# Attention's first unit: a fourth pair of score banks, and the third half of scores ahead of the feed-forward's last transposes

## The reference

```python
x = x + 0.5 * ffn(layernorm(x))
x = x + attention(layernorm(x))
x = x + 0.5 * ffn(layernorm(x))

# ffn: 8 experts, the best 2 of each token by sigmoid score plus bias, and a shared expert
h      = square(relu(score * (xf @ w_up.T)))     # hidden width 176 for each expert
hs     = square(relu(xf @ shared_w_up.T))
out    = sum of the two experts' h @ w_down.T + hs @ shared_w_down.T

# attention: one head, 4096 fixed keys and values
q      = hidden @ Wq.T + bq
scores = q @ memory_keys.T / sqrt(128)
probs  = softmax(scores)
out    = (probs @ memory_values) @ Wo.T + bo
```

## Time and profile before

| | us |
|---|---|
| median of 3 runs | 653.56 |
| the three runs | 653.99, 653.56, 652.54 |
| the profiled execution, its own time | 654.36 |
| its span, first to last instruction | 652.6 |

### The profile page before, as it was taken

One profiled execution on the slowest core, in us unless ns is written; L12 is line 12 of the kernel. 1 busy time (PEld: TensorE's weight loads), 2 busy tenths in 40 slices (PEclk: granted clock), 3 DMA queues, 4 the chain that ended last, 5 costly groups with the idle time before them and its releaser, 6 DMA issues.

```text
span 652.6 us, 9400 instructions
## 1 busy us (share of the span) xinstructions
PE 612.6 (94%) x2868; PEld 432.5 (66%) x2884; DVE 531.6 (81%) x944; ACT 455.9 (70%) x765; POOL 398.3 (61%) x443
## 2 busy tenths in 40 slices
PE   7799998798989999999999999999999988999997
PEld 4455544576767777777777777777777766645543
DVE  5889886886967978988887897897898858699885
ACT  3577787474757777777777776777776765567886
POOL 4987670462565966867677587596677787524100
PEclk9899999899989999999999999999999999999999
DMA  8021210425264373653735727447355360000000
GB/s 308 6 64 34 65 33 1 113 58 137 59 153 102 92 162 86 141 118 81 174 82 129 158 61 170 95 99 171 81 138 109 87 130 1 1 17 17 33 32 33
DMA packets 35857, 59.19 MB, mean 91 GB/s; under 512 B 9056, under 2 KB 9696, under 8 KB 35680
## 3 DMA queue, kind: packets, MB, share of 16 engines
q1 hardware_dynamic: 31936, 53.34, 34.2%
q10 hardware_dynamic: 3360, 4.21, 2.5%
q0 software_dynamic: 512, 1.05, 0.6%
HBM read 8.23 MB, written 2.10 MB: 16 GB/s over the span
## 4 chain that ended last, share of the span: by engine, by line
PE 64%; DVE 19%; issue 5%; ACT 4%; SPq 3%; POOL 2%; DMA 1%; ACTq 1%; DVEq 0%; POOLq 0%
PE banks L1400 7%; PE banks L1402 7%; PE banks L1401 7%; PE banks L1441 6%; PE banks L1443 6%; PE banks L1442 6%; PE banks L1261 4%; DVE bank_max L1123 4%; PE banks L1420 4%; PE banks L1252 4%; DVE probsT L1019 4%; DVE E L1118 3%; SPq L351 3%; PE banks L1451 2%; PE banks L1271 2%
## 5 line engine op out<-in xcount | busy, mean ns | idle before, releaser
L551 POOL TENSOR_TENSOR p_lo<-probsT,p_hi 128x768 fp32r<-128x768 f32 (+1 forms) x128 | 226.9, 1776 | 129.1 <-ACT p_hi L759 128.7
L1123 DVE TENSOR_REDUCE bank_max<-banks 128x1 f32<-128x1024 f32 x128 | 156.0, 1219 | 33.4 <-PE banks L1402 32.4
L1400 PE MATMUL banks<-kv_lo,q_parts 128*128 128x512 f32 x256 | 112.4, 439 | 10.2 <-ACT E L781 5.1
L759 ACT ACTIVATE p_hi<-probsT 128x768 fp32r<-128x768 f32 (+1 forms) x128 | 104.3, 816 | 24.0 <-PE banks L1443 21.1
L1118 DVE STREAM_TRANSPOSE E<-E 128x1024 f32<-128x1024 f32 x92 | 113.5, 1234 | 3.8 <-ACT E L781 3.8
L1019 DVE SCALAR_TENSOR_TENSOR probsT<-banks,E 128x1024 bf16<-128x1024 f32 x80 | 95.3, 1217 | 21.5 <-PE banks L1252 21.4
L781 ACT ACTIVATE E<-banks,neg_max 128x1024 f32<-128x1024 f32 x92 | 102.4, 1113 | 12.6 <-DVE neg_max L1129 6.7
L661 ACT ACTIVATE probsT<-probsT 128x1024 bf16<-128x1024 bf16 x96 | 92.5, 982 | 22.8 <-DVE probsT L1019 18.4
L1441 PE MATMUL banks<-p_hi,kv_lo 128*128 128x512 f32 x256 | 108.1, 422 | 0.3 <-issue 0.3
L1442 PE MATMUL banks<-p_lo,kv_hi 128*128 128x512 f32 x256 | 102.7, 401 | 0.0
L1443 PE MATMUL banks<-p_hi,kv_hi 128*128 128x512 f32 x256 | 102.7, 401 | 0.0
(11 more groups left out here) (128 smaller groups left out, 888.5 us busy)
## 6 DMA issues: line engine op xcount, KB each, us to landing
probsT<-E SPq DMA_DIRECT2D x224, 128.0 KB, 2.4
probsT<-E SPq DMA_DIRECT2D x208, 64.0 KB, 2.0
E<-in_keys_values SPq DMA_DIRECT2D x8, 512.0 KB, 3.5
probsT<-E ACTq DMA_DIRECT2D x64, 64.0 KB, 2.3
out<-X SPq DMA_DIRECT2D x8, 256.0 KB, 2.0
X<-in_x SPq DMA_DIRECT2D x1, 1280.0 KB, 9.4
probsT<-E POOLq DMA_DIRECT2D x16, 64.0 KB, 2.5
X<-in_x SPq DMA_DIRECT2D x3, 256.0 KB, 5.8
```

The costliest lines, as they stand in the source:

```text
L551: pool.tensor_tensor(moved_part(p_lo, ring), moved_pair(ring // UP, ring % UP), moved_part(p_hi, ring).bitcast(fp32), ALU.subtract).then_i ...
L759: act.activation(moved_part(p_hi, ring), moved_pair(ring // UP, ring % UP), ACT.Copy).then_inc(moved_hi_done, 1)
L1123: dve.tensor_reduce(bank_max[:, i % 2, h:h + 1], score_pair(u, i, h).rearrange("p b n -> p (b n)"), AX.X, ALU.max).then_inc(bank_max_done, 1)
L1400: pe.matmul(bank, qh, kl, start=True, stop=False)
```

## The change

In unit 0 the halves go round four pairs of banks, in the order 0, 1, 3, 2. From unit 1 on they go round three as before, from another place of the round. Up to half 9 a half waits until p - 3 exponentials are done, later ones until p - 2. Half 2, now in the gate and xT banks, is computed at the end of ffn(0) ahead of transpose_back, and waits for the last weighting on VectorE (which reads the gate bank) and the last copy of the spread weights on ScalarE (which reads the xT bank). Half 3, now in the y and z banks, takes over the wait for the residual. On VectorE the residual is written at the start of step 2 where it was at the end of step 1.

```diff
         def score_pair(u, i, h):
 
-            p = (2 * (u * GT + i) + h) % SCORE_PAIRS
+            half = 2 * (u * GT + i) + h
+            p = (0, 1, 3, 2)[half % (SCORE_PAIRS + 1)] if u == 0 else (half + 1) % SCORE_PAIRS
             return banks[:, 2 * p:2 * p + 2, :]
...
                     if ring is not None:
                         own_low(ring)
+                    if u == 0 and h == 2:
+                        residual(GROUPS - 1, GROUPS - 1)
                     if u < UNITS:
                         maximum(u, h // 2, h % 2)
...
                         transpose_squares(at_u, at_h // 2, at_h % 2)
-                    if u == 0 and h == 1:
-                        residual(GROUPS - 1, GROUPS - 1)
...
                 down(down_last, 4)
                 down(down_last, 5)
+                if f == 0:
+                    scores(0, 1, 0)
                 transpose_back(base + GROUPS - 1)
...
                 p = 2 * (u * GT + i) + h
-                wait(pe, exp_done, p - SCORE_PAIRS + 1)
+
+                wait(pe, exp_done, p - SCORE_PAIRS + (0 if p < HALVES + 2 else 1))
                 if p == 2:
-
+                    pe.wait_ge(weighted, GROUPS * SLOTS)
+                    pe.wait_ge(wbc_copied, GROUPS)
+                if p == 3:
                     pe.wait_ge(x_updated, GROUPS)
                     pe.wait_ge(yT_copied, GROUPS)
...
-                    if u < UNITS and H >= 2:
+                    if u < UNITS and H >= 3:
                         scores(u, h // 2, h % 2)
```

## The result

The changed kernel takes 649.50 us in the median (647.83 to 650.79, 5 runs), the kernel before 653.54 (651.34 to 653.99, 5 runs). The ratio is 0.9948 with a 95% interval of 0.9925 to 0.9971. That is 4.0 us less where 3.4 were forecast, 0.7 us under the forecast time.

What follows compares the result with a forecast made beforehand. VectorE was taken to bound the head, standing still before half 2 and where three pairs are too few. 1.37 + 0.60 + 0.80 + 0.66 = 3.43, taken as 3.4 us off 653.56, gives 650.2 us; 8-in-10 range 649.2 to 652.1.

Steps and rivals of the forecast that it cites:

- Half 2 ahead of the transposes: End of ffn(0): scores of half 2 computed before the last transposes let its maximum on VectorE start 1.37 us earlier.
- VectorE's edit: Residual moved from the end of step 1 to the start of step 2: order unchanged, costs and gives nothing.
- Halves 7 and 9: VectorE's idles of 0.73 and 0.59 us before these maxima go with four pairs of banks: 0.80 and 0.66 us.
- Half 5: VectorE's idle of 0.53 us before this maximum goes with four pairs of banks: 0.60 us gained.
- The clock ahead of half 8: TensorE's clock may fall after its 1.65 us wait there, making half 8 0.4 us late; within the forecast's own range.
- The strips: Unit 0's last strips might make moved_high(0) on ScalarE wait 0 to 0.7 us; 0 taken, 0.7 kept for the range.
- Behind half 10: After 136 us everything moves by the same 3.4 us, with nothing taken back and nothing extra.
- a growing wait on strips in units 1 to 3: Sign of being wrong: a wait on strips there grows by what the head gained.
- Only the move pays: Rival: the fourth pair gives nothing in the head, only half 2's move gains, 1.37 us, time 652.2; chance 0.12.
- Given back: Rival: a transfer not tied to the head, from 147 to 192 us, absorbs the gain, time 653.6; chance 0.06.
- slower: Rival: clock falls of 1.7 us each from 136 us on; two cancel the gain, three give 655.3; chance 0.05.

Runs made afterwards that it cites:

- e8: The kernel before, with two unused matmuls in TensorE's wait ahead of half 5; half 0 to half 10 took 24.04 us, ratio to before 0.9978.
- e2: The changed kernel, but each half waits for the exponential three before, as with three pairs; half 0 to half 10 took 22.67 us, ratio to before 0.9968.
- e1: The changed kernel with VectorE's residual written back at the end of step 1; half 0 to half 10 took 21.05 us, ratio to before 0.9948.
- e4: The changed kernel, but half 2 computed behind the last transposes without waiting for the residual; half 0 to half 10 took 21.36 us, ratio to before 0.9959.
- e3: The changed kernel, but half 2 computed behind the last transposes and waiting for the residual; half 0 to half 10 took 23.60 us, ratio to before 0.9982.
- e11: The changed kernel once more, unchanged; half 0 to half 10 took 21.05 us, median 649.53 us, ratio to before 0.9945.
- e9: The kernel before once more, unchanged, for a second trace; half 0 to half 10 took 24.75 us, from there to the end 517.7 us.
- e5: The changed kernel with an extra, unused maximum of half 2 on VectorE ahead of the real one; half 0 to half 10 took 22.17 us, ratio to before 0.9973.

## Why the prediction was right, point by point

The head's account, all from half 0's maximum to half 10's: 24.7 us before; 24.04 with the clock kept whole (e8); 22.67 with the move as well (e2, whose clock is whole here); 21.05 with the fourth pair in full (e1). So the clock is worth 0.65 us, the move 1.37 and the fourth pair 1.62: 3.64 us in all, against 3.43 summed. The clock's part is in both traces of the kernel before; how many of its other executions have it isn't known.

- *Half 2 ahead of the transposes, 1.37 us.* Right. Against half 0's maximum, half 2's went from 6.32 us to 4.99: 1.33. The transposes ended at 112.76 where the kernel before has them at 112.68, but on a time scale that is 0.44 earlier, so they are 0.5 us later, as priced; half 3 was ready in time. e4 adds what the prediction did not separate: banks of its own give 1.06 us of it, the place in the order 0.3.
- *VectorE's edit, nothing.* Right (e1).
- *Halves 7 and 9, 0.80 and 0.66 us.* Right in mechanism and place: e2 brings back exactly these two idles. Together 1.62 us, where 1.46 was summed. Half 9 gave what was summed for it: its maximum comes 3.00 us behind half 8's in e2 and 2.33 in the changed kernel, 0.67 less. From half 6 to half 8 it is 3.32 and 2.42 us, 0.90 less where 0.80 was summed, and the last 0.05 is spread over the other halves.
- *Half 5, 0.60 us.* The size was right and the reason wrong, so that this term came out by luck. I put its idle down to the three pairs and named the clock beside it. e2 and e8 show that the clock made all of it: a wait on a bank of the same kind (1.57 us in e2) costs VectorE nothing when half 5 runs at full rate. The fourth pair therefore bought nothing at half 5; the move alone (e2) already removed this idle. With the change the wait at this place goes from 2.20 us to 0.33, and no trace of the changed kernel has the fall there. That the shorter wait is the reason isn't shown: the last section has longer waits without a fall and shorter ones with it.
- *The clock ahead of half 8.* The wait came out at 1.63 us, 1.65 worked out, and the clock did not fall there in any trace of the changed kernel (three, and six of variants with a fourth pair in use); e2 with waits of 1.57, 1.64 and 1.34 us kept it too, while 2.20 us cost it in both traces of before. The Trainium skill (TensorE: Matmul & The Clock Gate, the table of the two states) gives the lower clock as the state behind an idle window. These traces don't agree: in both traces of before, and in e3, scores had just begun again at the full rate when it came (rows at 120.15 in the earlier trace rows, 119.98 and 113.78 above).
- *The strips, 0 to 0.7 us.* None paid: moved_high(0) followed the exponential ahead of it at once, with all strips in. SP's last strip was issued at 127.9, 2.2 us ahead, where I had 2.4. The shortest landing was 2.1 us and the longest 2.8, so it was close: a last strip that took as long as the longest would have made moved_high(0) wait.

```profile
130.12 1.14 ACT L760 ACTIVATE p_hi<-probsT 128x512 fp32r<-128x512 f32 x2
```
```profile
L352 SPq DMA_DIRECT2D probsT<-E x16: 582/595/623, 118.3 to 127.9; - x16
...
DMA to landing us min/median/max: 2.1/2.6/2.8
```

- *Behind half 10, nothing.* Right as far as it can be told. The stretch to the end was 519.0 and 517.7 us in two traces of the kernel before, 518.0, 518.6 and 515.7 in three of the changed kernel. Of the 2.9 us by which the last three differ, 2.4 lie between the maxima of halves 24 and 28: 16.1 and 16.2 us in the first two, 13.7 in e11. Below are these maxima, the first matmul of half 27 between them and the busy time by stretch, for the changed kernel's first trace and then for e11:

```profile
176.31 1.21 DVE L1124 TENSOR_REDUCE bank_max<-banks 128x1 f32<-128x1024 f32 x1
...
192.42 1.22 DVE L1124 TENSOR_REDUCE bank_max<-banks 128x1 f32<-128x1024 f32 x1 [0.57 <-PE banks L1408]
```
```profile
186.14 0.50 PE L1406 MATMUL banks<-kv_lo,q_parts 128*128 128x512 f32 x1 [2.47 <-ACT E L782]
```
```profile
188.00:192.00 4.00, 4.00 (x15) 3.10 (x15) 2.96 (x4) 1.91 (x5) 3.73 (x3) 0.71 0.29 66
```
```profile
176.86 1.21 DVE L1124 TENSOR_REDUCE bank_max<-banks 128x1 f32<-128x1024 f32 x1
...
190.60 1.22 DVE L1124 TENSOR_REDUCE bank_max<-banks 128x1 f32<-128x1024 f32 x1 [0.16 <-PE banks L1408]
```
```profile
185.84 0.50 PE L1406 MATMUL banks<-kv_lo,q_parts 128*128 128x512 f32 x1 [1.64 <-ACT E L782]
```
```profile
188.00:192.00 4.00, 4.00 (x21) 3.15 (x20) 3.81 (x6) 2.85 (x5) 3.75 (x4) 1.00 0.22 50
```

The exponential that TensorE waits for there waited itself for strips (a DMA in both traces), 3.56 and 2.42 us. So 0.8 of the 2.4 us (2.47 against 1.64) are strips that came sooner, and the other 1.5 or so go with a fall of the clock that e11 doesn't have. The kernel before shows the same pair: 16.3 us with the fall in its first trace, behind a wait of 2.66 us, and 14.3 without it in e9, behind 2.24. The prediction named a growing wait on strips in units 1 to 3 as a sign of being wrong; this one, in unit 3, did not grow (2.66 and 2.24 us before, 2.47, 2.59 and 1.64 with the change). The 1.0 us by which the first pair differed behind half 10 isn't this fall, since both have it; its cause stays open. With the 0.44 us ahead of half 0 it is why the first two spans differ by 5.0 us where the head explains 3.6. That the head's gain reaches the end is told best by time: the changed kernel's three ratios (0.9948, 0.9948, 0.9945) are 3.4 to 3.6 us, and in all eleven measurements (the first and the ten with a ratio above) the gain by ratio, 1.2 to 4.2 us, is within 0.8 us of the head's, 0.6 to 4.0.
- *The rivals.* "Only the move pays" fell with e2. The Trainium skill's practical note (same page, HAM oscillation), that for one kernel double-buffering PSUM gave no further gain, doesn't carry over to this one: here one more pair gave 1.62 us, since two waits on banks stood in the path. "Given back" fell with the ratios just told and with e5 beside them, and "slower" with the measured time: in the stretch right behind the head, 136 to 147 us, the clock is 1.00 in all three traces of the changed kernel. The next fall, near 187 us, is in two of the three, as it is at 192 us in one of the two of before. One such fall cost about 1.5 us, the rival's estimate being 1.7.

## What to carry to other kernels

Where an idle has two possible makers, too few buffers and a slow producer, look at the producer's clock in the same rows before the price goes to the buffers: half 5's idle was named after scores in both traces of before, and only e2 and the filled wait told the two makers apart. Measure a small change of a long program between two landmarks of one engine near it: here they repeat within 0.1 us where the spans of three traces of one program differ by 2.1 us, and the parts of a change can then be added up. When two spans of one program differ, compare the granted clock stretch by stretch first. A producer's first job in a new stage can go into a buffer whose last user is done, ahead of the old stage's tail; here the buffer gave more (1.06 us) than the order (0.3).

## What was not expected of the hardware

TensorE's granted clock fell from 2.4 to 1.2 GHz behind a wait of 2.20 us in both traces of the kernel before, and not behind the waits of 1.62 to 1.64 us ahead of half 7 or 8 in the others. From the head alone the length of the wait seems to decide, but the rest of the traces doesn't bear that out. Ahead of half 27 the clock stayed whole behind waits of 2.23 and 2.24 us (e8 at 189.21, e9 at 189.94) and fell around the end of one of 1.96 (e5, at 186.71). Near 28 us the changed kernel kept its clock in two traces and lost it in the third (e11), at the same wait of 1.53 or 1.54 us each time. In e3 it fell at half 2, after waits of 0.69 and 0.99 us with only transposes between them, at a place where the kernel before kept its clock in both traces with waits of 0.69 and 0.83 us. So the same instructions don't always meet the lower clock, and what decides it stays open.

Such a fall is worth 0.65 us at half 5, 1.0 us at half 2 and about 1.5 us at half 27. Two matmuls of no use in the wait went with a whole clock in the one trace taken, and made the kernel before faster by 0.2% (0.9978, 0.9963 to 0.9994).
